# Eight tiles of the first mixture of experts move into the end of the first attention; the root of group 15 stands in front of eight scatters

## The reference, cut to what matters

```python
x = x + _L0_gnn_ref(_layernorm(x, axis=-1), adj, ...)
x = x + _L0_ffn_ref(_layernorm(x, axis=-1), ...)
# in _L0_ffn_ref:
att = jax.nn.softmax(scores, axis=-1)
y = jnp.einsum('bhts,bhsd->bhtd', att, v).transpose(0, 2, 1, 3).reshape(Bx, Tx, Cx)
x = x + y @ wo.T
flat = _rmsnorm(x, ln2_w).reshape(-1, Cx)
probs = jax.nn.softmax(flat @ router_w.T, axis=-1)
tp, ti = jax.lax.top_k(probs, TOPK)          # 2 of 8 experts
tp = tp / (jnp.sum(tp, axis=-1, keepdims=True) + 1e-09)
for e in range(NE):                          # w1, w3: 128 to 341, w2: 341 to 128
    hh = jax.nn.silu(flat @ w1[e].T) * (flat @ w3[e].T)
    out = out + weights[:, e:e + 1] * (hh @ w2[e].T)
```

## Time and profile before

| | |
|---|---|
| median of 3 runs | 1419.8 us (1419.68 to 1421.0) |
| profiled execution, its own time | 1417.62 us |
| its span, first to last instruction | 1415.8 us |
| mean granted TensorE clock | 0.909 of 2.4 GHz |
| PE, DVE, ACT, POOL busy | 1150.4, 998.1, 673.5, 863.3 us |
| first attention's last scatter starts | 559.44 us |
| first transpose of the experts | 565.80 us |

### The profile page before, as it was taken

How to read it: one execution, slowest core, us unless ns; L and a number is a source line. 1 busy time by engine, 2 the same in 40 slices (tenths; PEclk the granted TensorE clock), 3 DMA queues, 4 the chain that set the end, 5 groups by cost and what they waited for, 6 DMA issues and landing times. The chain is left out here.

```text
span 1415.8 us, 33178 instructions
## 1 busy us (share of the span) xinstructions
PE 1150.4 (81%) x9205; PEld 953.8 (67%) x9205; DVE 998.1 (70%) x3983; ACT 673.5 (48%) x1725; POOL 863.3 (61%) x741
## 2 busy tenths in 40 slices
PE   6999998767777741999999993877774199999996
PEld 4776676557666741888888882545443199989996
DVE  4999999888888844577767664787885355566554
ACT  5766666357777731333333331333332154555453
POOL 3567676554477676344444441167777478888887
PEclk9999999889999975999999997777785599999998
DMA  6400000000011112666565663244332245555553
GB/s 189 67 2 2 1 2 2 1 1 17 28 36 41 40 49 79 191 191 203 187 204 189 199 210 120 62 119 127 119 118 65 79 63 69 71 65 68 73 68 45
DMA packets 126255, 122.61 MB, mean 87 GB/s; under 512 B 16577, under 2 KB 108097, under 8 KB 126129
## 3 DMA queue, kind: packets, MB, share of 16 engines
q1 hardware_dynamic: 92720, 85.65, 21.5%
q0 software_dynamic: 32960, 35.36, 12.8%
q10 hardware_dynamic: 448, 0.10, 0.0%
HBM read 76.71 MB, written 44.34 MB: 85 GB/s over the span
## 5 line engine op out<-in xcount | busy, mean ns | idle before, releaser
L2847 POOL DMA_INDIRECT out<-m_yb,m_dsti x142 | 227.9, 1605 | 62.5 <-DVE m_yb L2947 29.4
L2148 POOL DMA_INDIRECT rows<-m_yb,m_dsti x135 | 129.6, 960 | 169.3 <-DVE m_dsti L2279 145.6
L2224 ACT ACTIVATE m_sg<-psum 128x256 f32<-128x256 f32 (+3 forms) x216 | 79.8, 369 | 178.3 <-PE psum L2177 174.0
L1375 POOL DMA_INDIRECT dispatch<-g_flat,g1r_pos x128 | 129.2, 1009 | 45.6 <-issue 33.7
L1117 POOL DMA_INDIRECT dispatch<-common_v,a1r_pos x128 | 125.1, 978 | 47.4 <-issue 35.0
L2177 PE MATMUL psum<-m_xT,m_w 128*128 128x256 f32 (+3 forms) x648 | 140.3, 366 | 0.7 <-ACT m_xT L2215 0.7
L2920 ACT ACTIVATE m_hT<-psum,m_w 128x256 f32<-128x256 f32 (+1 forms) x240 | 92.8, 447 | 99.7 <-PE psum L2874 98.7
L2177 PEld LDWEIGHTS psum<-m_xT,m_w 128*128 128x128 f32 (+1 forms) x648 | 106.2, 178 | 18.3 <-ACT m_xT L2215 0.9
L2885 PE MATMUL psum<-m_w,m_hT 128*128 128x128 f32 x848 | 105.7, 277 | 3.9 <-DVE m_yb L2943 3.9
L2874 PE MATMUL psum<-m_xT,m_w 128*128 128x256 f32 (+1 forms) x480 | 103.2, 358 | 1.0 <-issue 0.8
L2885 PEld LDWEIGHTS psum<-m_w,m_hT 128*128 128x128 f32 x848 | 100.2, 193 | 4.5 <-issue 3.7
(11 more groups left out here) (314 smaller groups left out, 3048.0 us busy)
## 6 DMA issues: line engine op xcount, KB each, us to landing
m_w<-in_c_wall SPq DMA_DIRECT2D x54, 533.0 KB, 3.4
ahead_w<-in_c_wall SPq DMA_DIRECT2D x18, 533.0 KB, 3.6
g1c_y<-rows SPq DMA_DIRECT2D x32, 256.0 KB, 3.4
m_xg<-dispatch SPq DMA_DIRECT2D x47, 132.0 KB, 3.4
m_xg<-dispatch SPq DMA_DIRECT2D x46, 130.0 KB, 2.2
resident<-in_c_wall SPq DMA_DIRECT2D x8, 578.0 KB
out<-x SPq DMA_DIRECT2D x16, 256.0 KB
out<-m_yb,m_dsti POOLq DMA_INDIRECT x142, 3.3
```

The lines of the kernel that those rows point to most:

```text
L1375: pool.indirect_dma_start(out=dest, out_offset=bass.IndirectOffsetOnAxis(ap=self.pos[t % 3][:, k, p:p + 1], axis=0), in_=flat[:, p, :], in ...
L2148: pool.indirect_dma_start(out=rows_out, out_offset=bass.IndirectOffsetOnAxis(ap=dsti[j][:, t:t + 1], axis=0), in_=yb[j][:, t, :], in_offse ...
L2224: act.activation(sg[j % 2][0:cn, k, 0:rows], up_banks[j % 2][k][0:cn, 0:rows], ACT.Silu)\
L2847: pool.indirect_dma_start(out=out_rows, out_offset=bass.IndirectOffsetOnAxis(ap=dsti[j][:, t:t + 1], axis=0), in_=yb[j][:, t, :], in_offse ...
```

## The change

`EARLY = 8` full tiles are run by the new class `Early` inside the last steps of the attention, and `phase_experts` is left with 64 tiles (55 full ones). Their table is made in step 13 (`vector_table`, 20 operations), from the counts after groups 0 to 9; they are full tiles of rows that are in the list by then. SyncE loads weights and rows into four sets of buffers: the one there was before (`ahead.w`) and space that the graph attention and the attention have done with. The fourth set waits for the scores of group 15, each later tile for the result of the tile four before. Steps 16 to 19 are replaced on four engines by a written-out order (`end_step`) in which the eight tiles are mixed with the attention's rest. Their results stay in `common_s` and `common_pt` until `phase_experts`, where GpSimd stores them, two more indirect DMAs behind each of the first eight tiles' own. `roots(16)` moves from behind 12 scatters to in front of them, `pos` gets a third buffer. The table is cut in two: `vector_counts` (21 operations) comes behind the ranks of the last batch and the shares of tile 5, `vector_places` (12) between tiles 6 and 5. `ahead` also waits for the fifth result, since `ahead.w` is used by tiles 0 and 4.

```diff
+EARLY = 8
+FULL1, TILES1 = FULL - EARLY, TILES - EARLY
...
+EARLY_BATCH = [first + n for first, n in BATCHES].index(10 * PG)
...
         dve.wait_ge(*s.now(t, 3))
-        self.wait_landed(dve, t - 2)
-        dve.tensor_copy(self.pos[t % 2][:, :, 0:n], self.posf[:, :, 0:n]).then_inc(s.sem, 1)
+        self.wait_landed(dve, t - 3)
+        dve.tensor_copy(self.pos[t % 3][:, :, 0:n], self.posf[:, :, 0:n]).then_inc(s.sem, 1)
...
-    links = 28
+    links = 32
...
+        then(dve.tensor_tensor(tf[:, :], tf[:, :], used[:, 0:NE], ALU.subtract))
+        then(dve.tensor_tensor(th[:, :], th[:, :], twice[:, 0:NE], ALU.subtract))
...
+        then(dve.tensor_tensor(step[:, :, :], step[:, :, :],
+                               bass.AP(change, 0, [change[:, :].ap[0], [0, 2], [1, NE]]), ALU.add))
+        self.linked = n[0]
+
+    def vector_places(self, dve, c, early):
...
+class Early:
...
+        self.w_up = [self.ahead.w[:, 0:W2], k0[:, 0:W2], k1[:, 0:W2], a_q[:, 0:W2]]
+        self.w_down = [self.ahead.w[:, W2:NW], k0[:, W2:NW], k1[:, W2:NW], a_k[:, 0:NW - W2]]
...
+    def vector_table(self, dve, counted):
...
+        then(dve.tensor_scalar(T.cneg[:, :], rev[:, :], float(CAP), float(-NE * CAP), ALU.mult, ALU.add))
+        then(dve.tensor_tensor(T.ti[:, :], base[:, :], T.cneg[:, :], ALU.add))
+        then(dve.tensor_scalar(T.tj[:, :], T.ti[:, :], TILE.bit_length() - 1, None, ALU.logical_shift_right))
...
+        then(dve.tensor_tensor(self.change[:, :], self.twice[:, 1:NE + 1], self.twice[:, 0:NE], ALU.subtract))
...
+    def sync(self, sp, R, scored):
+
+        sp.wait_ge(self.chain, self.links)
+        for j in range(EARLY):
+            at = sp.value_load(self.table[0:1, 0, j:j + 1], min_val=0, max_val=NE * (CAP // HALF) - 2)
+            ex = sp.value_load(self.table[0:1, 1, j:j + 1], min_val=0, max_val=NE - 1)
+            if j == 0:
+                R.wait_landed(sp, EARLY_BATCH)
+            if j == 3:
+                sp.wait_ge(*scored)
+            if j >= 4:
+                sp.wait_ge(self.y_ready, j - 3)
+            wall = self.wall[bass.ds(ex, 1), :, :].rearrange("a p n -> p (a n)")
+            sp.dma_start(self.w_up[j % 4], wall[:, 0:2 * HID1]).then_inc(self.loaded[j % 4], 16)
+            sp.dma_start(self.w_down[j % 4], wall[:, 2 * HID1:]).then_inc(self.loaded[j % 4], 16)
+            sp.dma_start(self.xg[j % 4], self.halves[bass.ds(at, 2), :, :].rearrange("a p c -> p a c")).then_inc(self.loaded[j % 4], 16)
...
+    def tensor_x(self, pe, j):
+        self.here(pe, j)
+        if j >= 1:
+            pe.wait_ge(self.xT_ready, j)
+        for t in range(2):
+            i = pe.transpose(self.bX[:, 128 * t:128 * t + 128], self.xg[j % 4][:, t, 0:C], self.c["ident"][:, :])
+        i.then_inc(self.x_done, 1)
+
+    def tensor_up(self, pe, j):
+        pe.wait_ge(self.xT_ready, j + 1)
+        for k, (c0, cn) in enumerate(CH1):
+            if j >= 1:
+                pe.wait_ge(self.h_ready, len(CH1) * (j - 1) + k + 1)
+            for m in range(2):
+                i = pe.matmul(self.up_banks[k][0:cn, TILE * m:TILE * m + TILE], self.w_up[j % 4][:, HID1 * m + c0:HID1 * m + c0 + cn],
+                              self.xT[j % 2], start=(m == 0), stop=True, skip_group_check=True)
+            i.then_inc(self.up_done, 1)
+    def tensor_down(self, pe, j):
+        pe.wait_ge(self.h_ready, len(CH1) * (j + 1))
+        if j >= 1:
+            pe.wait_ge(self.y_ready, j)
...
+    def scalar_silu(self, act, j):
+        for k, (c0, cn) in enumerate(CH1):
+            act.wait_ge(self.up_done, len(CH1) * j + k + 1)
+            if j >= 1:
+                act.wait_ge(self.h_ready, len(CH1) * (j - 1) + k + 1)
+            act.activation(self.sg[0:cn, k, :], self.up_banks[k][0:cn, 0:TILE], ACT.Silu).then_inc(self.act_done, 1)
+    def vector_h(self, dve, j):
+        for k, (c0, cn) in enumerate(CH1):
+            dve.wait_ge(self.act_done, len(CH1) * j + k + 1)
+            if j >= 2:
+                dve.wait_ge(self.down_done, j - 1)
+            dve.tensor_tensor(self.hT[j % 2][0:cn, k, :], self.up_banks[k][0:cn, TILE:2 * TILE], self.sg[0:cn, k, :], ALU.mult)\
...
+    def vector_y(self, dve, j):
+        dve.wait_ge(self.down_done, j + 1)
+        dve.wait_ge(self.share_ready, 6 * j + 6)
...
+        def end_step(g, b):
+            if g == GROUPS:
+                out_T(g - 1)
+                E.tensor_x(pe, 0)
+                R.tensor_rank(pe, batch_due(g, 4), bR)
+                out_product(g - 1)
+                E.tensor_up(pe, 0)
+                flat_T(g - 2, (b - 2) % 4)
+                E.tensor_x(pe, 1)
+                E.tensor_up(pe, 1)
+                logits(g - 2)
+                E.tensor_x(pe, 2)
+                E.tensor_down(pe, 0)
+            elif g == GROUPS + 1:
+                E.tensor_up(pe, 2)
+                E.tensor_x(pe, 3)
+                R.tensor_rank(pe, batch_due(g, 4), bR)
+                flat_T(g - 2, (b - 2) % 4)
+                E.tensor_down(pe, 1)
+                E.tensor_up(pe, 3)
+                logits(g - 2)
+                E.tensor_x(pe, 4)
+                E.tensor_down(pe, 2)
...
+        def end_step(g, b, h):
+            if g == GROUPS:
+                t = batch_due(g, 4)
+                out_T(g - 1)
+                E.scalar_x(act, 0)
+                R.scalar_exp(act, t, batch_rows(flat, t))
+                out_flat(g - 2, h - 1, (b - 2) % 4)
+                E.scalar_silu(act, 0)
+                out_squares(g - 1)
+                flat_T(g - 2)
+                E.scalar_x(act, 1)
+                E.scalar_silu(act, 1)
+                E.scalar_x(act, 2)
...
+        def end_rows(t):
+            R.vector_rows(dve, t, bR)
+            R.vector_z(dve, t, batch_rows(flat, t))
+
+        def end_step(g):
+            if g == GROUPS:
+                end_rows(batch_due(g, 4))
+                out_x2(g - 1)
+                E.vector_share(dve, 0)
+                E.vector_h(dve, 0)
+                out_ms(g - 1)
+                E.vector_share(dve, 1)
+                E.vector_h(dve, 1)
+                t = batch_due(g, 3)
+                R.vector_choose(dve, t, bR, batch_rows(flat, t))
+                E.vector_y(dve, 0)
...
+            elif g == GROUPS + 2:
+                E.vector_share(dve, 4)
+                E.vector_h(dve, 4)
+                end_rows(batch_due(g, 4))
+                E.vector_y(dve, 3)
+                E.vector_share(dve, 5)
+                E.vector_h(dve, 5)
+                T.vector_counts(dve, c, state["base"], R.pstep.now(LAST_BATCH, 4), E)
+                E.vector_y(dve, 4)
+            elif g == GROUPS + 3:
+                E.vector_share(dve, 6)
+                E.vector_h(dve, 6)
+                T.vector_places(dve, c, E)
+                E.vector_y(dve, 5)
+                E.vector_share(dve, 7)
+                E.vector_h(dve, 7)
+                E.vector_y(dve, 6)
+                E.vector_y(dve, 7)
...
+            if g == GROUPS - 3:
+                E.vector_table(dve, R.pstep.now(EARLY_BATCH, 4))
...
-            roots(g)
+            if g < GROUPS:
+                roots(g)
+            elif g == GROUPS:
+                roots(g + 1)
             t, u = batch_due(g, 4), batch_due(g, 5)
             if u is not None and BATCHES[u][1] == PB:
-                R.pool_scatter(pool, u, 6, 16, batch_rows(flat, u), dest)
+                if g == GROUPS - 1:
+                    R.pool_scatter(pool, u, 6, 12, batch_rows(flat, u), dest)
+                    roots(GROUPS)
+                    R.pool_scatter(pool, u, 12, 16, batch_rows(flat, u), dest)
...
-        T.vector(dve, c, state["base"], R.pstep.now(LAST_BATCH, 4))
+        pass
...
+        E.sync(sp, R, pe_s.now(GROUPS - 1, 1))
         T.sync(sp, c, dest)
+        sp.wait_ge(E.y_ready, EARLY - 3)
         ahead.sync(sp, "m1", T, R, wall, dest)
...
+                        if isinstance(g, int) and g * UN + j < EARLY:
+                            n = g * UN + j
+                            for t in range(2):
+                                pool.indirect_dma_start(
+                                    out=rows_out, out_offset=bass.IndirectOffsetOnAxis(ap=E.dsti[:, n, t:t + 1], axis=0),
+                                    in_=E.y[n][:, t, :], in_offset=None).then_inc(early_stored, 16)
+                for g in range(EARLY // UN):
+                    body(g)
+                turns(pool, EARLY // UN, LIKE, body)
```

231 lines of the change are left out of this document (197 added, 34 removed).

## The result

| | before | changed |
|---|---|---|
| median | 1420.4 us (4 runs, 1419.68 to 1421.63) | 1402.1 us (4 runs, 1400.87 to 1409.73) |
| profiled execution, its own time | 1417.62 us | 1401.14 us |
| granted TensorE clock, mean | 0.909 | 0.917 |
| first transpose of the experts | 565.80 us | 576.53 us |

The ratio is 0.9887, 95% interval 0.9861 to 0.9912; a second set of five runs gave 0.9877 (0.9857 to 0.9898). 1399 was forecast, in 1393 to 1411.

A forecast was written before the change was run, and what follows sets the result against it. GpSimd's queue bounds the attention's end, TensorE the expert stage. Eight tiles -33.2, later stage begin +11.9, late_add +0.5 sum to -20.8 us: 1396.8 from 1417.62, or 1399 against 1419.8; range 1393 to 1411.

The forecast's parts named there:

- Eight tiles less: Expert stage: eight full tiles removed at 4.15 us each, 33.2 us less.
- `late_add` on the half tiles: Expert stage: eight half tiles carry an extra add on VectorE, 0.5 us more, bounds 0 and 2.3.
- The early table: Step 13, VectorE: twenty chained operations, 4.4 us, make what follows 2.5 us late; bounds 0 and 4.4.
- The slack of 1.90: VectorE behind the early table: out_ms(12)'s 1.90 us wait for ScalarE's squares is used up first, leaving 2.5 us late.
- `roots(16)` and `out_flat(14)`: Attention's end: GpSimd waits until 516.0 for the moved root; ScalarE's out_flat(14) can start at 523.5, not 528.17.
- VectorE's chain: Attention's end: VectorE's remaining work of 36.5 us plus 3 of waits runs from 535.9 to 575.4.
- The terms for shares and products: VectorE's work for tiles 2 to 7: shares at 1.21 us each, 7.3; three products with Silu per tile, 7.2.
- The barrier: Between attention and experts: 2.3 us after VectorE's last result, so the expert stage begins at 577.7, 11.9 us later.
- No longer last: Attention's end: GpSimd's queue ends at 563.9 instead of 560.4, ahead of VectorE's last result.
- GpSimd falls behind: Rival, first eight expert tiles: stores take 5.04 against 4.15 us; if not hidden, up to 7.1 us, 1406; chance 0.07.
- The switches: Rival, ScalarE at the attention's end: five table switches at some 2.6 us each add 5 to 7, 1404 to 1406; chance 0.15.
- The clock: Rival, TensorE at the attention's end: half clock throughout gives +2.0 us, 1422, chance 0.04; half of it, chance 0.1.

The follow-up runs named there:

- stores_mid: The changed kernel with the 16 stores of the early tiles in one piece behind the first four own tiles; median 1412.40 us, ratio 0.9937.
- silu_first: The changed kernel with ScalarE's Silu of tile 0 and the squares of group 15 in front of out_flat of group 14; median 1403.08 us, ratio 0.9863.
- stores_first: The changed kernel with the 16 early tiles' stores in one piece ahead of the loop and all turns in the loop again; median 1396.20 us, ratio 0.9827.
- one_table: The changed kernel with Silu in place of the last two batches' exponentials (probabilities wrong), leaving out four of five table loads; median 1404.15 us, ratio 0.9882.

## Why the prediction was right, and where its sizes were off

**Eight tiles less.** -33.76 us in the experts against -33.2 + 0.5 forecast. `late_add` on the half tiles cost nothing that shows: in the ten profiles of kernels with the same tiles (all but `stores_mid`) the stretch was 257.4 to 259.8 us, a spread larger than the term.

**The early table.** This term was sized too small. From R, `roots(15)` came at 29.80 and 29.48 us against 25.95: 3.5 to 3.9 us for 4.7 us of table (488.59 to 493.27), not 2.5. The slack of 1.90 was used up as forecast: the `a_pin` behind the table came 2.8 us later from R (16.09 against 13.27), which is 4.7 less 1.9. The rest wasn't in the sum. At the next `a_pin` (29.25 against 25.69) VectorE stood 0.83 us for ScalarE's squares, which it didn't before, and GpSimd waited 0.72 and 1.38 us for landings just ahead of `roots(15)`. The `a_pin` of `roots(16)` was 3.6 late, inside the bounds of 0 and 4.4.

**`roots(16)` and `out_flat(14)`.** `roots(16)` stood 10.31 us behind `roots(15)`, forecast 10.3. It came 2.28 later than forecast: 0.92 from ahead of R, 1.12 from the table, and 0.24 for `a_pin`'s own operation, which the forecast left out. `out_flat` came at 525.87, 2.4 later than forecast. From there the working held: 5.66 us to up of tile 1 (6.0 forecast), and 6.1 to the logits' end (6.4 forecast).

**VectorE's chain.** It began at 537.65, 1.8 us after the forecast, and gave the last result at 574.64, 0.8 us before it: 37.0 us for 39.5. The terms for shares and products were too large: a share of a tile takes 0.87 in its place (541.00 to 541.87), not 1.21, and three products 1.00, not 1.2; for six tiles that is 3.2 us. The last down at half clock took 2.90, not the 1.4 forecast, since TensorE had waited 2.87 us for result 5, which stands behind the second part of the table. The other waits (1.28 at 545.13, 0.29 and 0.31 for Silu) came to 1.9 us, forecast 3.

**The barrier.** 1.9 us from the last result to the first transpose, 2.3 forecast. The 2.3 had been read where GpSimd's drain (1.45 us, from 562.15) stood ahead of the barrier; VectorE's end has no such drain.

**GpSimd.** "No longer last" was right, but only just: its drain ended at 573.1, 1.6 us ahead of the last result. The last scatter started at 568.19 instead of 563. 2.3 of the 5.2 us came from the late `roots(16)`; a gap of 2.14 us at 549.30 that nothing in the trace releases, and landings that were waited for, three of them for 0.57 to 0.88 us, gave the rest. `silu_first` shows how close it is.

**The step that failed** is the one that isn't in the prediction: the end of the experts was taken as unchanged. The rival "GpSimd falls behind" counted its stores in time, found them hidden (and they were: 257.46 us for the experts with all 16 in front), and saw nothing at the end of its queue. The drain cost 6.3 us; without it the profiled execution would be at 1395, and `stores_first` is at 1396.2. The time fell into the range because the errors partly cancelled: -2.1 us in the attention, -1.1 in the experts, +6.3 at their end, and +1.2 in stretches that the change doesn't touch leave +4.3.

**Rivals.** The switches: five loads of 1.28 with nothing behind them, and four of them worth at most some tenths on VectorE's chain. By the Trainium skill (ScalarE: Activation LUTs, What ACT_TABLE_LOAD costs) a switch takes about 2.66 us; an estimate from that page, with half of four switches on the chain, is a gain of over 5 for `one_table`. The traces agree on the load's own length, 1.28, but show no drain behind it, and no such gain. The clock: half under up of tile 1, full in 545 to 560, low again for down of tile 7 and the first own tile. Low through the whole tail didn't happen in any profile. One execution of the changed kernel took 1409.73; no profile of it exists, and its cause is open.

## What to carry to other kernels

Work that is moved out of a stage with a full engine saves its whole length there (33.8 us here), and costs in its new place only what the last two queues to finish don't hide. Find both of them: here they stood 2 us apart, and the second capped what a further edit on the first could give. A cap also hides what an edit is worth, so measure the edit on its own chain (`one_table`). A stage's end has a price of its own, which here changed with the order of GpSimd's stores: after any change to that queue compare the time from the last result to the next phase. Placing a value earlier for somebody (the root) can give nothing alone and 7.6 of 19.3 us together with what uses it, so test such halves both ways.
